# Reordering waits, passes and transposes in a fused graph and LSTM kernel

## What is computed

```python
h = relu(layernorm(x))
# layer 0
h = relu(adj @ (h @ Wg0 + bg0)); h = relu(adj @ (h @ Wg1 + bg1))
for p in range(1, 5):
    # windows of p neighbouring tokens; an LSTM with weights of its own runs over each window
    # and its last state replaces the window's last token
    last = lstm_last(Wih[p-1], Whh[p-1], bih[p-1], bhh[p-1], windows(h, p))
    h[:, p-1::p] = last
x = x + h
# layer 1
h = relu(layernorm(x))
z = (A_hat @ h) @ W1.T + b1            # A_hat: adj with self loops, scaled by 1/sqrt(degree)
z2 = relu(batchnorm(z)) @ W2.T + b2    # both batch norms over all 16 * 512 tokens
x = x + batchnorm(z2)
```

## Time and profile before

| | us |
|---|---|
| median of 3 runs (lowest, highest) | 544.71 (543.46, 546.0) |
| the profiled execution | 545.15 |
| its span, first to last instruction | 541.9 |
| PE busy in the span | 508.4 (94%) |
| DVE busy | 414.9 (77%) |
| ACT busy | 352.2 (65%) |
| POOL busy | 175.5 (32%) |
| mean granted PE clock | 0.991 |

### The profile page before, as it was taken

How to read it: one execution, slowest core, us unless ns; L and a number is a source line. 1 busy time by engine, 2 the same in 40 slices (tenths; PEclk the granted TensorE clock), 3 DMA queues, 4 the chain that set the end, 5 groups by cost and what they waited for, 6 DMA issues and landing times.

```text
span 541.9 us, 8009 instructions
## 1 busy us (share of the span) xinstructions
PE 508.4 (94%) x2712; PEld 432.0 (80%) x2712; DVE 414.9 (77%) x952; ACT 352.2 (65%) x676; POOL 175.5 (32%) x293
## 2 busy tenths in 40 slices
PE   7998998899998999999989999999899998798996
PEld 5687876798887889899878898989677998675565
DVE  4687688878968978677579886775887888877966
ACT  3644765557668677576677775766867786447944
POOL 4504021304400854163006560530033414246520
PEclk9999999999999999999999999999989999999999
DMA  7302000000001122001111101010920000600008
GB/s 241 111 20 99 0 1 19 9 13 21 1 19 68 30 79 74 5 21 58 59 58 41 59 19 59 2 59 1 369 78 20 21 1 21 222 13 0 2 0 310
DMA packets 17452, 31.20 MB, mean 58 GB/s; under 512 B 1498, under 2 KB 6020, under 8 KB 17284
## 3 DMA queue, kind: packets, MB, share of 16 engines
q1 hardware_dynamic: 16420, 30.17, 16.4%
q10 hardware_dynamic: 992, 0.52, 0.4%
HBM read 19.16 MB, written 11.53 MB: 57 GB/s over the span
## 4 chain that ended last, share of the span: by engine, by line
PE 55%; DVE 24%; ACT 9%; issue 6%; POOL 3%; POOLq 1%; DMA 1%; DVEq 0%; ACTq 0%
PE gate_ps L1158 10%; PE gate_ps L1160 10%; PE gate_ps L1159 10%; PE pre_ps L1159 4%; PE pre_ps L1160 4%; PE pre_ps L1158 4%; PE post_ps L1158 3%; PE post_ps L1160 3%; PE post_ps L1159 3%; ACT gate L704 3%; ACT gate L691 2%; DVE cell L987 2%; DVE cell L982 2%; PE pre_ps L1224 2%; DVE hstep_lo L803 1%
## 5 line engine op out<-in xcount | busy, mean ns | idle before, releaser
L691 ACT ACTIVATE gate<-gate_ps,gate_bias 128x256 f32<-128x256 f32 (+2 forms) x312 | 164.5, 563 | 42.1 <-PE gate_ps L1160 39.6
L1158 PE MATMUL gate_ps<-by_class_hi,wih_hi 128*128 128x256 f32 (+2 forms) x264 | 86.1, 326 | 4.6 <-DVE by_class_lo L803 4.3
L1160 PE MATMUL gate_ps<-by_class_lo,wih_hi 128*128 128x256 f32 (+2 forms) x264 | 84.5, 320 | 0.0
L1159 PE MATMUL gate_ps<-by_class_hi,wih_lo 128*128 128x256 f32 (+2 forms) x264 | 84.4, 320 | 0.0
L429 POOL TENSOR_TENSOR by_class_lo<-h,by_class_hi 128x256 fp32r<-128x256 f32 (+1 forms) x40 | 35.1, 876 | 137.3 <-ACT by_class_hi L702 137.3
L704 ACT ACTIVATE gate<-cell 128x512 f32<-128x512 f32 (+2 forms) x88 | 45.5, 517 | 46.0 <-DVE cell L982 32.0
L1158 PE MATMUL gate_ps<-hstep_hi,whh_hi 128*128 128x256 f32 (+2 forms) x192 | 60.8, 317 | 3.0 <-DVE hstep_lo L803 3.0
L1160 PE MATMUL gate_ps<-hstep_lo,whh_hi 128*128 128x256 f32 (+2 forms) x192 | 60.2, 313 | 0.0
L1159 PE MATMUL gate_ps<-hstep_hi,whh_lo 128*128 128x256 f32 (+2 forms) x192 | 60.1, 313 | 0.0
L1158 PEld LDWEIGHTS gate_ps<-by_class_hi,wih_hi 128*128 128x128 f32 x264 | 50.6, 192 | 10.6 <-DVE by_class_lo L803 6.2
L1159 PEld LDWEIGHTS gate_ps<-by_class_hi,wih_lo 128*128 128x128 f32 x264 | 50.7, 192 | 3.8
(11 more groups left out here) (304 smaller groups left out, 1270.3 us busy)
## 6 DMA issues: line engine op xcount, KB each, us to landing
x_pre<-in_x SPq DMA_DIRECT2D x16, 256.0 KB, 2.6
x<-in_x SPq DMA_DIRECT2D x16, 256.0 KB, 2.6
z_spill<-z_ring SPq DMA_DIRECT2D x8, 512.0 KB, 2.9
z_back<-z_spill SPq DMA_DIRECT2D x8, 512.0 KB, 7.0
x_spill<-x SPq DMA_DIRECT2D x12, 256.0 KB, 2.0
x_back<-x_spill SPq DMA_DIRECT2D x1, 3072.0 KB, 12.0
out<-x_back SPq DMA_DIRECT2D x12, 256.0 KB, 2.0
x<-in_adj SPq DMA_DIRECT2D x1, 1024.0 KB, 5.2
```

Of the source, the lines that this page charges most:

```text
L691: nc.scalar.activation(gate[:, tile_of(g), gt, 0:size], gate_ps[k % GATE_BANKS][:, 0:size], ACT.Tanh if gt == G_GATE else ACT.Sigmoid, bia ...
L1158: nc.tensor.matmul(ps, w[0], m[0], start=start, stop=False)
L1159: nc.tensor.matmul(ps, w[1], m[0], start=False, stop=False)
L1160: return nc.tensor.matmul(ps, w[0], m[1], start=False, stop=stop)
```

## The change

It has six parts.

1. **Hi ahead of lo.** `product` takes an optional semaphore that PE waits for only ahead of its third matmul. The first gate of a turn now waits for the hi part of its input (`class_hi`, `later_hi`) and of its state (`step_hi`), and for the lo parts ahead of the third matmul.
2. **A_hat between cell and state.** The blocks of `hat_chunk` are cut into four steps (add and diagonal; scale; hi; lo), one step in each of the slots 5 to 20, and they stand inside the turn, between the cell and the wait for its tanh.
3. **POOL helps in round 3.** It writes the low part for p = 1 of chain 0 (g66, g67) instead of DVE, and the even tokens of all four p = 1 turns (g66 to g69) instead of ACT. DVE's write of a cell two turns later and PE's third matmul wait for it (`pool_lo`).
4. **Transposes first.** In each slot PE does "turn" ahead of the pre units, and DVE its `turned` ahead of their low parts.
5. **Layer 1's end recast.** Whole batches are k = 0, 1, 3, ..., 13; four sums instead of six stay in PSUM; the final transposes use four PSUM banks instead of two, and the first batch goes through scale, transpose, add and store in two halves.
6. **Banks 12 and 13 earlier.** In the prologue bank 12 comes ahead of (AGG1, 2) and bank 13 ahead of the norm of batch 4 and (AGG1, 3).

```diff
-                    + [(LIN1, 3), ("bank", 11), ("deg", DEG_DIAG), (AGG1, 2), ("bank", 12)]
+                    + [(LIN1, 3), ("bank", 11), ("deg", DEG_DIAG), ("bank", 12), (AGG1, 2), ("bank", 13)]
                     + [(kind, n) for kind, n in IN_PROLOGUE if kind == "norm"]
-                    + [(AGG1, 3), ("bank", 13)])
+                    + [(AGG1, 3)])
...
+POOL_LO = [g for g in range(N_TURNS) if TURNS[g][0] == ROUNDS - 1 and TURNS[g][2] == 1 and TURNS[g][1] == 0]
+POOL_EVEN = [g for g in range(N_TURNS) if TURNS[g][0] == ROUNDS - 1 and TURNS[g][2] == 1]
+SUMS = 4
-WHOLE = tuple(range(0, BATCHES, 2))
-KEPT_Z2 = tuple(range(BATCHES - GATE_BANKS, BATCHES))
-DVE_Z2 = (2, 5, 8)
+WHOLE = (0,) + tuple(range(1, BATCHES - 2, 2))
+KEPT_Z2 = tuple(range(BATCHES - SUMS, BATCHES))
+DVE_Z2 = (3, 6, 9)
-DVE_HALVES = ((1, 0), (1, 1))
+DVE_HALVES = ((2, 0), (2, 1))
+def pieces(k):
+    return [slice(0, T // 2), slice(T // 2, T)] if k == 0 else [slice(0, T)]
-        fin_ps = [pre_ps, post_ps]
+        fin_ps = [pre_ps, post_ps, gate_ps[SUMS], gate_ps[SUMS + 1]]
...
+                if slot in POOL_LO:
+                    pool.wait_ge(class_hi, CLASS_AT[r, chain, 1, sub])
+                    hi, lo = (part[:, chain, :].rearrange("h (t b) -> h t b", b=SUBS)[:, :, sub] for part in by_class)
+                    nc.gpsimd.tensor_tensor(lo, cell[:, tile_of(slot), :], f32(hi), ALU.subtract).then_inc(pool_lo, 1)
+                if slot in POOL_EVEN:
+                    pool.wait_ge(h_done, slot + 1)
+                    pool.wait_ge(turn_mm, batch_of(r - 1, chain, sub) + 1)
+                    nc.gpsimd.tensor_copy(h32[:, chain, 0::2, sub], cell[:, tile_of(slot), 0:T // 2]).then_inc(even_done, 1)
...
+                    if PREV[g] in POOL_LO:
+                        dve.wait_ge(pool_lo, POOL_LO.index(PREV[g]) + 1)
...
+                if HAT_FROM <= g < HAT_FROM + 4 * CHUNKS:
+                    hat_step((g - HAT_FROM) // 4, (g - HAT_FROM) % 4)
                 dve.wait_ge(tanh_ready, g + 1)
...
-            def product(ps, w, m, start, stop):
+            def product(ps, w, m, start, stop, lo_made=None, count=0):
                 nc.tensor.matmul(ps, w[0], m[0], start=start, stop=False)
                 nc.tensor.matmul(ps, w[1], m[0], start=False, stop=False)
+                if lo_made is not None:
+                    pe.wait_ge(lo_made, count)
                 return nc.tensor.matmul(ps, w[0], m[1], start=False, stop=stop)
...
-                        pe.wait_ge(later_lo, LATER_CLASS_AT[r, chain, p, step])
+                        lo_made, made = later_lo, LATER_CLASS_AT[r, chain, p, step]
+                        pe.wait_ge(later_hi, made)
                     else:
-                        pe.wait_ge(class_lo, class_count(r, chain, p))
+                        made = class_count(r, chain, p)
+                        pe.wait_ge(class_hi, made)
...
-                            pe.wait_ge(step_lo, STEP_AT[PREV[g]])
+                            pe.wait_ge(step_hi, STEP_AT[PREV[g]])
...
                 lstm_turn(slot)
                 deg_steps(slot)
-                for kind, n in PRE_AFTER[slot]:
-                    if kind in SPLITS:
-                        pre_unit(kind, n, pre_ps, 0)
                 for kind, n in POST_AFTER[slot]:
                     if kind == "turn":
...
                         turn(n, turn_ps(n))
-                    elif kind == "agg":
+                for kind, n in PRE_AFTER[slot]:
+                    if kind in SPLITS:
+                        pre_unit(kind, n, pre_ps, 0)
+                for kind, n in POST_AFTER[slot]:
+                    if kind == "agg":
```

More of the change, by code:

```diff
@@ L80, with lo_count @@
         CLASS_AT[_r, _chain, _p + 1, 0] = len(CLASS_AT) + 1
+POOL_LO = [g for g in range(N_TURNS) if TURNS[g][0] == ROUNDS - 1 and TURNS[g][2] == 1 and TURNS[g][1] == 0]
+POOL_EVEN = [g for g in range(N_TURNS) if TURNS[g][0] == ROUNDS - 1 and TURNS[g][2] == 1]
+POOL_CLASSES = [CLASS_AT[TURNS[g][0], TURNS[g][1], 1, TURNS[g][4]] for g in POOL_LO]
+def lo_count(made):
+    return made - sum(k <= made for k in POOL_CLASSES)
 N_STEPS = len(STEP_AT)
@@ L109, in count_to, with piece_number @@
     return sum(j <= k for j in some)
+def pieces(k):
+    return [slice(0, T // 2), slice(T // 2, T)] if k == 0 else [slice(0, T)]
+def piece_number(k, at):
+    return k + 2 if k > 0 or at.start > 0 else 1
 def halves_to(halves, k):
@@ L659, in agg_out @@
                 nc.scalar.activation(agg[i][0][:, :], ps[:, :], ACT.Copy).then_inc(agg_hi, 1)
-            def even_later(g):
-                r, chain, p, step, sub, nb = TURNS[g]
-                return p == 1 and r == ROUNDS - 1
             def even_tokens(g):
@@ L709, in _ @@
                 for splits in (True, False):
-                    if not splits and TURNS[slot][2] == 1 and not even_later(slot):
+                    if not splits and TURNS[slot][2] == 1 and slot not in POOL_EVEN:
                         even_tokens(slot)
@@ L785, in _ @@
                 zz = z_end(END_ORDER[k])
-                if k in KEPT_Z2:
+                if k == 0:
+                    for half in range(HALVES):
+                        z2, y = (zz[:, s:s + T].rearrange("p (t c) -> p c t", c=CHUNKS)[:, 2 * half:2 * half + 2, :]
+                                 for s in (0, T))
+                        nc.scalar.activation(y, z2, ACT.Identity, bias=bn2[:, 5, 0:1], scale=bn2[:, 4, 0:1])\
+                            .then_inc(y_act, 1)
+                elif k in KEPT_Z2:
                     if k == KEPT_Z2[0]:
@@ L1007, in lstm_turn @@
                     nc.vector.tensor_copy(hi, c_).then_inc(class_hi, 1)
-                    dve.wait_ge(class_hi, CLASS_AT[r, chain, 1, sub])
-                    low(lo, c_, hi).then_inc(class_lo, 1)
+                    if g not in POOL_LO:
+                        dve.wait_ge(class_hi, CLASS_AT[r, chain, 1, sub])
+                        low(lo, c_, hi).then_inc(class_lo, 1)
                 else:
@@ L1020, in _ @@
                 lstm_turn(slot)
+                for kind, n in POST_AFTER[slot]:
+                    if kind == "turn" and n not in IN_NEXT_TURN:
+                        turned(n, turn_ps(n))
                 for splits in (True, False):
@@ L1280, in lstm_turn @@
                 size = nb * (T // p)
+                lo_made, made = None, 0
                 if p == 1:
@@ L1297, in lstm_turn @@
                     ps = gate_ps[k % GATE_BANKS][:, 0:size]
-                    last = product(ps, [part[:, p - 1, gt, :] for part in wih], inputs, True, step == 0)
+                    last = product(ps, [part[:, p - 1, gt, :] for part in wih], inputs, True, step == 0,
+                                   lo_made if j == 0 else None, made)
                     if step > 0:
                         if j == 0:
-                            pe.wait_ge(step_lo, STEP_AT[PREV[g]])
+                            pe.wait_ge(step_hi, STEP_AT[PREV[g]])
                         last = product(ps, [part[:, p - 2, gt, :] for part in whh],
-                                       [part[:, chain, 0:size] for part in hstep], False, True)
+                                       [part[:, chain, 0:size] for part in hstep], False, True,
+                                       step_lo if j == 0 else None, STEP_AT[PREV[g]])
                     last.then_inc(gates_mm, 1)
```

92 lines of the change are left out of this document (51 added, 41 removed).

## The result

| | before | after |
|---|---|---|
| median (lowest to highest), us | 545.43 (543.46 to 546.58), 6 runs | 536.78 (536.64 to 538.10), 6 runs |
| profiled execution, its span | 545.15, 541.9 | 536.65, 534.5 |
| POOL busy, us | 175.5 | 185.8 |

The medians are 8.65 us apart, where 17.1 were forecast. The ratio of after to before is 0.9862 (95% interval 0.9841 to 0.9882), which is 7.5 us of 545 (6.4 to 8.7): in the later sets of runs the kernel before took 544.1 to 544.9 us, and beside it the changed kernel, measured again, took 536.38 against 544.12. So the gain is 7.5 to 8.65 us, half of the forecast or somewhat less. The time lies inside the range, at its slow end, and 9 us from the forecast itself (527.6).

A forecast was written before the change was run, and what follows sets the result against it. PE was taken as the bound, with time to win only in its waits, lower-clock stretches and the last 17 us. Terms 3.6 + 6.6 + 1.0 + 3.2 + 0.8 + 1.9 = 17.1 us gave median 527.6; range 522 to 537.

The forecast's parts named there:

- rival A: The loop from ACT through DVE to ACT takes freed PE waits back one turn later: 536.1 us, chance 0.18.
- The idle 1.87: Prologue's end: PE's 1.87 us wait for bank 13's low parts goes; 1.9 us, also part 6's lower bound.
- The 1.7 us for the slow stretch behind it: After the prologue: the stretch at granted clock 0.51 behind PE's idle time goes too, 1.7 us.
- The wait of 2.07 us and the stretch behind it: Round 0: PE's wait behind the second A_hat block goes, 2.07 us, and the slow stretch after it, 1.7 us.
- what is behind a step on DVE is its own turn's state: Round 0, A_hat steps: only that state stands behind a step, wanted by PE two turns later; within 6.6 us.
- PE is released for good by the third sum: Rounds 1 and 2, transposes first: PE keeps a net 0.5 us a round, 1.0 us in all.
- DVE loses two low parts: 1.4 us: Round 3: two low parts of about 0.69 us leave DVE for POOL, and PE gets the 1.4 us.
- The 1.0 us for later waits: Round 3: 0.3 at g75 and about four quarter-us waits for low parts in the last eight turns go.
- made behind two whole batches: Layer 1's end: first split batch is now third, its low part made behind two whole ones; gain 0.8 us.
- transfers then are the limit: Final stores: with four PSUM banks, 4.2 MB at 387 GB/s takes 10.8 us instead of 12.8; gain 1.9 us.
- C: POOL and DVE collide, stretching DVE by up to 3 us in round 3 and 2 in round 0: 532.6 us, chance 0.07.
- B: The slow-clock stretches show up elsewhere, giving 3.4 us back: 531.0 us, chance 0.12.

The follow-up runs named there:

- e6: Changed kernel with part 6 alone undone (banks 12 and 13 again behind the adjacency pass, the norm and the prologue's last adjacency pass): 538.74 us.
- e8: Changed kernel with POOL's seventh norm one slot later, behind the low part that g11's input needs: 535.81 us.
- e1: Changed kernel with part 1 alone undone, PE again waiting for low parts ahead of a group's first matmul: 537.51 us.
- e11: Changed kernel with eight filler matmuls on PE ahead of g71's wait and eight ahead of the tail's first hidden unit: 536.84 us.

## Why the prediction was right or wrong

**The sign** held; half of the size came, or less by the ratio (7.5 of 17.1). The order of the two largest terms, round 0 and part 6, was right. The sum failed because it priced each engine's queue by itself. What an engine loses while another works beside it stood at nothing in parts 2 and 3, and a gain of PE was taken as kept "for good" although DVE had moved back. That the time still lies inside the range is owed to rival A's price, not to A's mechanism.

**Part 6: 3.6 forecast, 2.0 measured.** The idle 1.87 was right. The 1.7 us for the slow stretch behind it failed: with the idle time back the clock stayed up in e6's profile, and the median moved by 2.0. The profile of before had the stretch, so it shows 3.8 us at g1. My own lower bound of 1.9 said what to take.

**Parts 2 and 1 in round 0: 6.6 forecast, some 4.5 to 5 measured** (4.5 and 0.7 us on PE, medians +4.0 and +0.7). The wait of 2.07 us and the stretch behind it went as forecast. The step that failed is "what is behind a step on DVE is its own turn's state": I followed the queue of DVE, and not POOL's, whose norm takes 4.08 instead of 2.38 us once the steps are moved, while a low part that PE wants waits behind it. e8 gets back 1.24 us on PE.

**Part 4: +1.0 forecast, -0.2 measured** on PE for two rounds. That the third transposes take back a part of what the fourth gain was forecast, 0.5 us net, and PE was 0.48 ahead. The low parts of the pre units cost nothing, as said. The step that failed is "PE is released for good by the third sum": layer 1's aggregation, which the prediction doesn't name, waits for a low part that DVE now makes 0.27 us later, and takes 0.58 back.

**Part 3 with part 1 in round 3: 3.2 forecast, 0.5 to 0.7 found.** POOL's 1.5 us for the subtraction was right in between (1.31 alone, 1.78 beside DVE). The term "DVE loses two low parts: 1.4 us" failed: it lost them and paid nearly the same in stretched products and casts. PE takes g71 0.9 us sooner by the high part than in e1, but that didn't last, since DVE decides when g72 can go on: in the eight profiles whose clock stays up behind g71, PE waits 0.91 to 0.95 us for the state there. The 1.0 us for later waits had no run of its own.

**Part 5: 0.8 and 1.9 forecast, about 0 to -0.5 and 0.8 measured.** The first failed at "made behind two whole batches": the waits for low parts went from 1.5 to 1.9 us instead of shrinking. Of the second, between DVE's first final addition, 526.94 - 518.29 = 8.65 us earlier, and the span's end, 7.4 us earlier, more than 1 us was lost. The additions came 0.60 apart as forecast, and "transfers then are the limit" held, at 380 GB/s where I took 387. But the transfers, which begin at 519.2 us, reach that rate only at 521.4, and I saw no code fetch among them, because before the fetch lay behind the end.

**The rivals.** Rival A named nearly the time (536.1). That is luck: its mechanism, the loop through ACT and DVE, took back little, since e8 gave PE 1.24 us and the loop left it all of it. C is the one that was there, at two places and with POOL as the loser at the dearer one; I had priced it at 5 us and given it 0.07. B was there by name, the slow stretches did move, but e11 shows that the two of 3.5 us in the changed kernel cost nothing. What I had not on any list is the end.

**The sum of the parts**, by the medians of the kernels with one part undone, is 2.0 + 4.0 + 0.7 - 1.2 + 1.85 - 0.5 + 0.8 = 7.65 of 8.65 us. By the ratios to before, which allow for the sets of runs, it is 2.2 + 3.3 + 0.2 - 1.6 + 0.8 - 0.2 + 0.9 = 5.6 of 7.5 us. Each term is uncertain by about 1 us, so only parts 2 and 6 are sure, and whether the parts add up to the whole is open.

## What to carry to other kernels

When a step moves on one engine's queue, price what runs beside it on the others at its new place: here an engine whose low parts had cost PE 0.2 us of waiting cost it 1.8, by contention and by the order of its own queue. A gain on one engine lasts only to the next place where it waits for another that has not gained with it. A stretch at the lower clock is worth its loss only where PE is what the others wait for, and a single profile doesn't tell that it belongs to the idle time before it. Once the last stage is as fast as its transfers, other traffic on the DMA engines can become part of the span.

## What the runs showed of the chip that I had not expected

- The contention between DVE and POOL can fall on either of them: beside each other, POOL's 128x512 subtraction took 1.78 us while DVE's product took 0.69, or 1.31 while DVE's took 1.21.
- In the changed kernel, whose last stores carried a 16 KB packet of instructions among them, the last packets landed one at a time for 1.1 us after all others, at a sixteenth of the rate.
- An idle PE of the same length (2.29 us) was followed by 3.5 us at 1.2 GHz in one kernel and by more than 6.5 in another with the same instructions there; eight matmuls of filler in it kept 2.4 GHz in both kernels that had them. At g71, idle times of 1.8 to 3.1 us were followed by the lower clock in 10 of 16 profiles.
